# Attention probabilities and values in f32 instead of split f16, and one relu and one square per step

## The reference

```python
queries, keys, values = (l2norm(queries), l2norm(keys), l2norm(values))
sim = jnp.einsum('bhid,bhjd->bhij', queries, keys)
attn = jnp.square(jax.nn.relu(sim))
aggr = jnp.einsum('bhij,bhjd->bhid', attn, values)
out = tanh_norm(aggr) * jnp.tanh(jax.nn.silu(gates))
return out @ Wout
```

## Time and profile before

| | |
|---|---|
| median of 3 runs | 3119.35 us (3118.72 to 3120.51) |
| span of the profiled execution | 3118.2 us |
| TensorE matmuls busy | 2774.7 us (89%), 15168 instructions |
| VectorE busy | 2549.5 us (82%), 5207 |
| ScalarE busy | 2288.4 us (73%), 4138 |
| GpSimd busy | 888.1 us (28%), 683 |
| TensorE's mean granted clock | 0.976 of full speed |

### The profile page before, as it was taken

How to read it: one execution, slowest core, us unless ns; L and a number is a source line. 1 busy time by engine, 2 the same in 40 slices (tenths; PEclk the granted TensorE clock), 3 DMA queues, 4 the chain that set the end, 5 groups by cost and what they waited for, 6 DMA issues and landing times.

```text
span 3118.2 us, 54633 instructions
## 1 busy us (share of the span) xinstructions
PE 2774.7 (89%) x15168; PEld 1174.7 (38%) x15168; DVE 2549.5 (82%) x5207; ACT 2288.4 (73%) x4138; POOL 888.1 (28%) x683
## 2 busy tenths in 40 slices
PE   2898998989989899998989989899898998989999
PEld 1343343333433344333433334333343333434433
DVE  8987879778687887878878788786987879888796
ACT  3787767778677786877868678686776867778686
POOL 0314123141332413224132231412314123141332
PEclk8999999999999999999999999999999999999999
DMA  3000000000000000000000000000000000000000
GB/s 154 7 1 21 1 22 1 1 22 1 22 1 1 22 1 22 1 1 22 1 22 1 1 22 1 22 1 22 1 1 22 1 22 1 1 22 1 14 1 8
DMA packets 19501, 40.23 MB, mean 13 GB/s; under 512 B 1584, under 2 KB 9904, under 8 KB 18128
## 3 DMA queue, kind: packets, MB, share of 16 engines
q1 hardware_dynamic: 19152, 36.11, 3.4%
HBM read 27.72 MB, written 8.39 MB: 12 GB/s over the span
## 4 chain that ended last, share of the span: by engine, by line
PE 40%; DVE 35%; issue 14%; ACT 7%; DVEq 2%; POOL 1%; ACTq 0%; DMA 0%; SPq 0%; POOLq 0%
PE wk L1104 18%; DVE pl L589 10%; PE acc L1104 10%; DVE ph L585 7%; PE av L1177 5%; DVE wide L505 2%; PE sim L1163 2%; ACT ring L899 2%; PE wk L1186 2%; DVE hf L609 2%; DVE vn_t L418 1%; ACT ring L903 1%; ACT sg L909 1%; PE wk L1228 1%; DVE vn_y L420 1%
## 5 line engine op out<-in xcount | busy, mean ns | idle before, releaser
L1056 POOL TENSOR_TENSOR hl<-hf,hh 128x512 f16<-128x512 f32 x288 | 369.5, 1283 | 1645.8 <-ACT hh L915 1482.0
L589 DVE TENSOR_TENSOR pl<-ring,ph 128x512 f16<-128x512 f32 x1024 | 759.9, 782 | 0.0
L899 ACT ACTIVATE ring<-sim 128x512 f32<-128x512 f32 x1024 | 567.5, 603 | 250.3 <-PE sim L1163 176.6
L903 ACT ACTIVATE ring<-ring 128x512 f32<-128x512 f32 x1024 | 593.6, 640 | 0.0
L585 DVE CAST ph<-ring 128x512 f16<-128x512 f32 x1024 | 472.0, 497 | 83.0 <-ACT ring L903 54.3
L1177 PE MATMUL av<-ph,vh 128*64 128x512 f16 x1024 | 211.7, 410 | 42.5 <-DVE pl L589 42.4
L609 DVE SCALAR_TENSOR_TENSOR hf<-wk,up_routed,sg 128x512 f32<-128x512 f32 x256 | 191.6, 749 | 66.9 <-PE wk L1104 16.3
L909 ACT ACTIVATE sg<-wk,inv_m 128x512 f32<-128x512 f32 x288 | 199.6, 693 | 46.6 <-PE wk L1104 46.4
L1077 POOL TENSOR_TENSOR pl<-wide,ph 128x512 f16<-128x512 f32 x128 | 169.6, 1329 | 211.4 <-ACT ph L947 211.4
L641 DVE TENSOR_TENSOR gate_sb<-gate_sb,wk 128x512 f32<-128x512 f32 x128 | 87.8, 686 | 162.9 <-PE wk L1228 162.7
L1104 PE MATMUL acc<-hh,down_h 128*128 128x512 f16 x576 | 220.2, 382 | 0.0
(11 more groups left out here) (192 smaller groups left out, 5386.4 us busy)
## 6 DMA issues: line engine op xcount, KB each, us to landing
x_sb<-x SPq DMA_DIRECT2D x16, 512.0 KB, 4.9
y_sb<-x_t SPq DMA_DIRECT2D x16, 512.0 KB, 4.3
out_t<-y_sb SPq DMA_DIRECT2D x16, 512.0 KB, 3.2
raw_wa<-wa SPq DMA_DIRECT2D x1, 2560.0 KB, 9.1
raw_gate<-w_gate SPq DMA_DIRECT2D x1, 2304.0 KB, 14.2
raw_up<-w_up SPq DMA_DIRECT2D x1, 2304.0 KB, 19.3
raw_down<-w_down SPq DMA_DIRECT2D x1, 2304.0 KB, 24.3
raw_wo<-w_out SPq DMA_DIRECT2D x1, 1024.0 KB, 26.1
```

The lines of the kernel that those rows point to most:

```text
L589: v.tensor_tensor(pl[:, n % NH_, :], ring[:, n % NR_, :], ph[:, n % NH_, :], ALU.subtract).then_inc(pl_done, 1)
L899: a(ring[:, n % NR_, :], sim[n % 2][:, :], ACT.Relu, scale=S_SCALE).then_inc(relu_done, 1)
L903: a(ring[:, n % NR_, :], ring[:, n % NR_, :], ACT.Square).then_inc(square_done, 1)
L1056: tt(hl[:, n % 2, :], hf[:, n % 2, :], hh[:, n % 2, :], ALU.subtract).then_inc(h_lo, 1)
```

## The change

The probabilities and the values stay f32. `ph` and `pl` become one f32 buffer `pr` of six tiles, `vh` and `vl` one f32 buffer `v32`, and the values product is one f32 matmul per head instead of three f16 ones. The copies to vh and the subtractions to vl are gone; VectorE's unit scaling writes v32. The two score tiles are one PSUM tensor of two banks; one relu on ScalarE reads both (1024 columns), and one multiplication on VectorE squares both into pr. The semaphores count steps instead of tiles. The buffers ah and al of the output stage, which were ph and pl, now lie in tiles 4 and 5 of pr.

```diff
-S_SCALE = 2.0 ** -7
-P_SCALE = 2.0 ** 14
-V_SCALE = 2.0 ** 8
+P_SCALE = QK_SCALE ** 4
...
-AG_UNSCALE = 1.0 / (P_SCALE * V_SCALE)
+AG_UNSCALE = 1.0 / P_SCALE
...
-        ph, pl = sb("ph", [P, NH_, T], F16), sb("pl", [P, NH_, T], F16)
+        pr = sb("pr", [P, NH_, T])
...
-        vh, vl = sb("vh", [P, NB, H * DV], F16), sb("vl", [P, NB, H * DV], F16)
+        v32 = sb("v32", [P, NB, H * DV])
...
-        sim = [ctx.enter_context(nc.psum_tensor(f"sim{n}", [P, T], F32)) for n in range(2)]
+        sim = ctx.enter_context(nc.psum_tensor("sim", [P, 2, T], F32))
...
-                v.scalar_tensor_tensor(out=blk, in0=blk, scalar=V_SCALE,
-                                       in1=vn_y[:, k, half * 8:half * 8 + 8].unsqueeze(2).to_broadcast([P, 8, DV]),
-                                       op0=ALU.mult, op1=ALU.mult).then_inc(vn_done, 1)
+                dve.wait_ge(av_step, upto(b, STEPS, 0))
+                v.tensor_tensor(v32[:, k, half * T:half * T + T].rearrange("p (h d) -> p h d", d=DV), blk,
+                                vn_y[:, k, half * 8:half * 8 + 8].unsqueeze(2).to_broadcast([P, 8, DV]),
+                                ALU.mult).then_inc(vn_done, 1)
...
-            def probs(b, n):
-
-                dve.wait_ge(square_done, upto(b, 2 * STEPS, n + 1))
-                dve.wait_ge(av_step, upto(b, STEPS, n // 2 - LAG))
-                if n < 4:
+            def square(b, s):
+
+                n, r = 2 * s % NH_, 2 * s % NR_
+                dve.wait_ge(relu_done, upto(b, STEPS, s + 1))
+                dve.wait_ge(av_step, upto(b, STEPS, s - LAG))
+                if s == 2:
                     dve.wait_ge(out_mm, upto(b, NP_, 0))
-                v.tensor_copy(ph[:, n % NH_, :], ring[:, n % NR_, :]).then_inc(ph_done, 1)
-
-            def probs_lo(b, n):
-                dve.wait_ge(ph_done, upto(b, 2 * STEPS, n + 1))
-                v.tensor_tensor(pl[:, n % NH_, :], ring[:, n % NR_, :], ph[:, n % NH_, :],
-                                ALU.subtract).then_inc(pl_done, 1)
+                v.tensor_tensor(pr[:, n:n + 2, :], ring[:, r:r + 2, :], ring[:, r:r + 2, :],
+                                ALU.mult).then_inc(square_done, 1)
...
-                    for n in (2 * s, 2 * s + 1):
-                        probs(b, n)
+                    square(b, s)
...
-                    for n in (2 * s, 2 * s + 1):
-                        probs_lo(b, n)
...
-            def relu(b, n):
-                act.wait_ge(sim_full, upto(b, 2 * STEPS, n + 1))
-                act.wait_ge(pl_done, upto(b, 2 * STEPS, n - NR_ + 1))
-                if n < NR_:
+            def relu(b, s):
+                r = 2 * s % NR_
+                act.wait_ge(sim_full, upto(b, STEPS, s + 1))
+                act.wait_ge(square_done, upto(b, STEPS, s - NR_ // 2 + 1))
+                if s < NR_ // 2:
                     act.wait_ge(qk_lo, upto(b, 2 * NB, 2 * NB))
-                a(ring[:, n % NR_, :], sim[n % 2][:, :], ACT.Relu, scale=S_SCALE).then_inc(relu_done, 1)
-
-            def square(b, n):
-                act.wait_ge(relu_done, upto(b, 2 * STEPS, n + 1))
-                a(ring[:, n % NR_, :], ring[:, n % NR_, :], ACT.Square).then_inc(square_done, 1)
+                a(ring[:, r:r + 2, :], sim[:, :, :], ACT.Relu).then_inc(relu_done, 1)
...
+                pe.wait_ge(relu_done, upto(b, STEPS, s))
                 for half in range(2):
-                    n = 2 * s + half
-                    pe.wait_ge(relu_done, upto(b, 2 * STEPS, n - 1))
                     rows = slice(64 * half, 64 * half + 64)
-                    mm(sim[half][:, :], kt[rows, pair, j * P:(j + 1) * P], qt[rows, pair, :], start=True,
-                       stop=True).then_inc(sim_full, 1)
+                    ins = mm(sim[:, half, :], kt[rows, pair, j * P:(j + 1) * P], qt[rows, pair, :], start=True,
+                             stop=True)
+                ins.then_inc(sim_full, 1)
...
-                pe.wait_ge(pl_done, upto(b, 2 * STEPS, 2 * s + 2))
+                pe.wait_ge(square_done, upto(b, STEPS, s + 1))
                 if pair == 0:
-                    pe.wait_ge(v_lo, upto(b, 2 * NB, 2 * (j + 1)))
+                    pe.wait_ge(vn_done, upto(b, 2 * NB, 2 * (j + 1)))
                 if j == 0:
                     pe.wait_ge(agg_done, upto(b, NP_, pair))
-                for i, (vv, pp) in enumerate(((vh, ph), (vl, ph), (vh, pl))):
-                    for half in range(2):
-                        h = 2 * pair + half
-                        ins = mm(av[64 * half:64 * half + 64, :], vv[:, j, h * DV:(h + 1) * DV],
-                                 pp[:, (2 * s + half) % NH_, :], start=(j == 0 and i == 0),
-                                 stop=(j == NB - 1 and i == 2))
+                for half in range(2):
+                    h = 2 * pair + half
+                    ins = mm(av[64 * half:64 * half + 64, :], v32[:, j, h * DV:(h + 1) * DV],
+                             pr[:, (2 * s + half) % NH_, :], start=(j == 0), stop=(j == NB - 1))
                 ins.then_inc(av_step, 1)
```

More of the change, by code:

```diff
@@ L250, in build_layer @@
         hh, hl = sb("hh", [P, 2, T], F16), sb("hl", [P, 2, T], F16)
-        ah, al = ph, pl
+        assert NH_ == 6
+        ah, al = (pr[:, n, :].bitcast(F16).rearrange("p (a t) -> p a t", a=2) for n in (4, 5))
         vn_a, vn_y, vn_t = (sb(f"vn_{c}", [P, NB, H]) for c in "ayt")
@@ L270, in build_layer @@
         sim_full, relu_done, square_done = sem("sim_full"), sem("relu_done"), sem("square_done")
-        ph_done, pl_done, av_step = sem("ph_done"), sem("pl_done"), sem("av_step")
+        av_step = sem("av_step")
         agg_done, agg_sq_done = sem("agg_done"), sem("agg_sq_done")
@@ L280, in build_layer @@
         k_turned = sem("k_turned")
-        v_hi, v_lo = sem("v_hi"), sem("v_lo")
         score_done, route_step, ct_done = sem("score_done"), sem("route_step"), sem("ct_done")
@@ L504, in unit_v @@
                 blk = v_raw[:, k, half * T:half * T + T].rearrange("p (h d) -> p h d", d=DV)
-                v.scalar_tensor_tensor(out=blk, in0=blk, scalar=V_SCALE,
-                                       in1=vn_y[:, k, half * 8:half * 8 + 8].unsqueeze(2).to_broadcast([P, 8, DV]),
-                                       op0=ALU.mult, op1=ALU.mult).then_inc(vn_done, 1)
+                dve.wait_ge(av_step, upto(b, STEPS, 0))
+                v.tensor_tensor(v32[:, k, half * T:half * T + T].rearrange("p (h d) -> p h d", d=DV), blk,
+                                vn_y[:, k, half * 8:half * 8 + 8].unsqueeze(2).to_broadcast([P, 8, DV]),
+                                ALU.mult).then_inc(vn_done, 1)
             def turned_q(b, k):
                 dve.wait_ge(work_full, filled(b, ("T", 2 * k)))
-                dve.wait_ge(sim_full, upto(b, 2 * STEPS, 0))
+                dve.wait_ge(sim_full, upto(b, STEPS, 0))
                 v.tensor_copy(qt[:, :, k * P:(k + 1) * P],
@@ L838, in raw @@
                 if n < NB:
-                    act.wait_ge(pl_done, upto(b, 2 * STEPS, 0))
+                    act.wait_ge(square_done, upto(b, STEPS, 0))
                     dst = qk_raw[:, n, :]
@@ L883, in turned_k @@
                 act.wait_ge(work_full, filled(b, ("T", 2 * k + 1)))
-                act.wait_ge(sim_full, upto(b, 2 * STEPS, 0))
+                act.wait_ge(sim_full, upto(b, STEPS, 0))
                 a(kt[:, :, k * P:(k + 1) * P], bank16(b, ("T", 2 * k + 1))[:, :].rearrange("p (m t) -> p m t", m=NP_),
                   ACT.Copy).then_inc(k_turned, 1)
[L888 to L892, removed]
-            def relu(b, n):
-                act.wait_ge(sim_full, upto(b, 2 * STEPS, n + 1))
-                act.wait_ge(pl_done, upto(b, 2 * STEPS, n - NR_ + 1))
-                if n < NR_:
+            def relu(b, s):
[3 more added lines that the diff above has]
+                if s < NR_ // 2:
                     act.wait_ge(qk_lo, upto(b, 2 * NB, 2 * NB))
-                a(ring[:, n % NR_, :], sim[n % 2][:, :], ACT.Relu, scale=S_SCALE).then_inc(relu_done, 1)
-            def square(b, n):
-                act.wait_ge(relu_done, upto(b, 2 * STEPS, n + 1))
-                a(ring[:, n % NR_, :], ring[:, n % NR_, :], ACT.Square).then_inc(square_done, 1)
+                a(ring[:, r:r + 2, :], sim[:, :, :], ACT.Relu).then_inc(relu_done, 1)
             def silu(b, e):
@@ L931, in take_heads @@
                 act.wait_ge(av_step, upto(b, STEPS, NB * (t + 1)))
-                act.wait_ge(v_lo, upto(b, 2 * NB, 2 * NB))
-                act.wait_ge(v_hi, upto(b, 2 * NB, 2 * NB))
+                act.wait_ge(vn_done, upto(b, 2 * NB, 2 * NB))
                 a(agg[:, t, :], av[:, :], ACT.Copy).then_inc(agg_done, 1)
@@ L977, in whole @@
                 expert_item(b, *HEAD[3])
-                split_hi_v(b, 0)
-                split_hi_v(b, 1)
                 turned_k(b, 3)
@@ L983, in whole @@
                         take_heads(b, s // NB - 1)
[L984 to L987, removed]
+                    relu(b, s)
```

(2 more changed lines are left out.)

6 lines of the change are left out of this document (removed).

## The result

| | us | ratio to before, 95% interval |
|---|---|---|
| before | 3119.93 (3118.72 to 3120.60) | |
| after | 3048.27 (3044.91 to 3052.51) | 0.9771 (0.9758 to 0.9785) |

A forecast was written before the change was run, and what follows sets the result against it. TensorE and VectorE were almost full in the step loop, TensorE needing most of the time itself. Per batch 107.7 + 20.2 + 1.9 replaced 123.5, less 0.6: +5.7 us, +91 in all, 3210 us; own range 3160 to 3270, 8-in-10 range 3150 to 3450.

The forecast's parts named there:

- three slots: Values group on TensorE: four f32 passes in 3 x 427 = 1281 ns, with form change 1.40 us, 0.63 more than before.
- the middle of three bounds: Two heads' f32 passes: 853 ns with full overlap, 1281 in queue order (taken), 1707 with none.
- the sign turned at 1.22 us: Values group length at which the change would neither gain nor lose, 0.45 us more than before.
- the same sum: Step loop per batch: 107.7 + 20.2 + 1.9 = 129.8 instead of 123.5 us, less 0.6 at the front.
- The wait at the start: Start of each batch's step loop: TensorE's third-step ct matmul waits 1.9 us for sg, behind VectorE's value scaling.
- the waits to be removed: TensorE's waits for VectorE (pl, hf, sg) inside the step loop, 10.2 us per batch.
- the floor: Step loop if TensorE never waits, before the longer values groups: 107.7 us per batch, 15.8 below the kernel before.
- the lower clock: Step loop: one 6.8 us stretch per batch at 1.2 instead of 2.4 GHz, costing 3.4 us, expected to go.
- The wait ahead of the first scores: Front of the step loop: kt, copied late behind a vh copy, delays the scores; some 0.6 us per batch saved.
- changing forms: TensorE's switch between matmul forms around a values group, 0.12 us per group, taken as unchanged.
- Rival D: Values group: one pass per f32 matmul, 0.55 us per group, 2775 us in all; chance 0.04.
- Rival A: Values group: full overlap of the two heads, 0.97 us per group, 2990 us in all; chance 0.12.

The follow-up runs named there:

- b_order: The kernel before with its six f16 values matmuls issued head by head instead of term by term; 3121.01 us, 1.0003 of before.
- a_pad32: The kernel after with 32 small matmuls put ahead of TensorE's first work; 3018.78 us, 0.9680 of before.
- a_pad64: The kernel after with 64 small matmuls put ahead of TensorE's first work; 3016.89 us, 0.9668 of before.
- a_best: a_pad32 with value blocks 2 to 7 scaled just ahead of the squares of steps 1 to 3 instead of ahead of step 0; 3022.83 us, 0.9692 of before.

## Why the prediction was wrong, point by point

The step that failed is "If matmuls start in order, B's first pass can start only with A's second: three slots", from which the middle of three bounds was taken. The measured group is 1.01 us, not 1.40. That is 0.39 x 512 = 200 us, and it turned the sign, since the sign turned at 1.22 us. b_order refutes the rule itself, on the f16 matmuls of the kernel before. My ground for it was that every "x2" row had its two heads next to each other in the queue; that was only how the queue happened to be written, and such rows can't tell order from independence. The Trainium skill (TensorE: Matmul & The Clock Gate, Part 3: Packing small matmuls) calls matmuls strictly first in, first out in start and end; b_order's rows differ from this across column halves (B's first term starts beside A's first, ahead of A's second and third), and the measurement decides.

With the measured group the same sum gives 3010 us. The 38 us up to 3048 are told by place from the two traces.

- In the step loops nothing is missing: 16 x 6.2 = 99 us less by that sum, 100 measured. But this agreement is in part luck, since errors cancel. The wait at the start was put at 1.9 us in every batch, 30 us in all; it measured 6.3 us in all, 24 the other way. (A value block takes 0.62 us rather than the 0.7 that I had taken, and my own terms for the first sg add up to 0.1 us more than the 1446.2 that I wrote.) Against it, the waits to be removed were 154 us and not 16 x 10.2 = 163, because the last batch has only 2.6. A step loop without a wait takes 116.0 us where the floor and the longer groups gave 107.7 + 32 x 0.24 = 115.4, 10 us in all. And the lower clock gave back 52 us, not 54.
- Outside them the forecast had 10 us less, and 27 more came. The once-per-turn gap, 13 x 2.0 = 26 us, was not in the sum; a_pad32 and a_pad64 measured 29 and 31. Nor was it in the sum that time at the lower clock would appear there: 40 us instead of 9, which costs 16. The trace has twelve such stretches between the first and the last step loop: nine begin within or right behind the 2.9 us wait for qt, just ahead of a step loop, and three right behind a once-per-turn gap. The wait for qt is in the kernel before too, where only two such stretches stand beside it; why they became frequent isn't shown. The wait ahead of the first scores gave 7 us, not 10, and the output projection's wait for GpSimd gave 5 us that were not in the sum; smaller terms make up the rest.

Only the group's length and the once-per-turn gap were tested by runs of their own; the other terms are read from one trace of each kernel.

What held: two passes per f32 matmul and two cycles per column (593 ns against 379); 0.12 us for changing forms was 1.01 - 0.853 = 0.16; VectorE's waits gone; the third step's sg as the one wait left, though in six batches only; and the floor of TensorE's work within 0.6 us. A step loop of the kernel after without a wait, which the floor puts at 115.4 us:

```profile
2147.50:2263.47 115.97, 115.97 (x567) 44.31 (x566) 80.61 (x139) 63.09 (x84) 17.06 (x15) 1.00 0.00 1
```

Rival D is refuted by the 2048 records. Rival A had a chance of 0.12 and was right in its mechanism; its 2990 lacked the once-per-turn gap and the clock outside the step loops, and had the group 0.04 us too short.

VectorE and ScalarE ended busier (69% and 56%) than forecast (60% and 47%). The forecast subtracted mean durations of neighbours that overlap by 0.04 to 0.06 us each (782 ns a subtraction, but 759.9 us busy in 1024 of them), the square's mean was 0.22 us over its median, and the shares are of a shorter span.

## What to carry to other kernels

When an edit trades one engine's time for another's, the sign hangs on how the new matmuls share the array, so measure overlap by reordering or by taking it away before counting slots. Two edits that remove the same wait don't add up: here f32 alone took what the width could have taken, and beyond that TensorE's work set the pace. Before you build on a wait that you read in one batch, ask for its total and its count over the whole execution: a_best was meant to gain 17 us from a wait that was worth 4.4 at most. In a loop, look for a gap that comes once per turn and that no engine ends: shifting the code by 64 or 128 instructions was worth 30 us.

## What the runs showed that was not expected

- Matmuls of one column half run beside later ones of the other half, although the queue holds them in another order: the group of six took 0.77 and 0.78 us in the two orders, and that of two f32 matmuls 1.01 us against 1.86 in the same half. Four f32 passes of one half behind four of the other took 1.87 us together.
- An f32 matmul of 128 by 64 by 512 costs 0.85 us of its columns' time, three f16 ones 0.65; with two heads side by side, the group costs 0.24 us more than the split one and, with the square moved to VectorE, saves VectorE some 1.1 us per step (2.56 against 1.45) and ScalarE 1.5.
- A once-per-turn gap of some 2 us that is there with 0 and 128 small matmuls ahead of the loop, and not with 32 and 64: 3048.27 and 3047.95 against 3018.78 and 3016.89 us.
- Once TensorE waited less in the step loops, its time at the lower clock there fell from 107 to 4 us, and outside them it rose from 9 to 40 us.
